# GpSimd waits behind each of the first three choices of a token scatter, not behind the second alone

## The reference

```python
shared = silu_and_mul(x @ shared_gate_up_w.T) @ shared_down_w.T
shared = shared * sigmoid(x @ sgate_w.T)
routing_weights = softmax(x @ gate_w.T)
topk_w, topk_ids = top_k(routing_weights, 4)
for e in range(16):
    coef = sum(where(topk_ids == e, topk_w, 0.0), axis=-1)
    h = silu_and_mul(x @ w13[e].T)
    acc = acc + (h @ w2[e].T) * coef[:, None]
out = shared + acc
```

## Time and profile before

| | us |
|---|---|
| median of 3 runs (lowest and highest) | 1221.72 (1220.41 to 1223.15) |
| the profiled execution: its own time | 1234.23 |
| the profiled execution: span from first to last instruction | 1232.4 |
| TensorE busy in the span | 1166.8 (95%) |
| GpSimd busy in the span | 601.7 (49%) |
| mean granted TensorE clock | 0.984 |

### The profile page before, as it was taken

How to read it: one execution, slowest core, us unless ns; L and a number is a source line. 1 busy time by engine, 2 the same in 40 slices (tenths; PEclk the granted TensorE clock), 3 DMA queues, 4 the chain that set the end, 5 groups by cost and what they waited for, 6 DMA issues and landing times.

```text
span 1232.4 us, 23046 instructions
## 1 busy us (share of the span) xinstructions
PE 1166.8 (95%) x7484; PEld 1003.6 (81%) x7484; DVE 806.7 (65%) x2038; ACT 752.4 (61%) x1734; POOL 601.7 (49%) x497
## 2 busy tenths in 40 slices
PE   6999999999988799988999999999999998989997
PEld 5888888888777577767999999999999996767775
DVE  7867667777784333377777777777777778533335
ACT  5866667666643233336878888888788776323331
POOL 3211222122116356633777766767676752745563
PEclk9999999999999899999999999999999999989999
DMA  3366766663246577651422222212222213666666
GB/s 116 88 175 176 182 156 170 189 172 68 68 147 237 160 132 137 124 122 39 88 76 60 74 62 60 60 62 66 60 66 72 49 47 108 230 210 116 111 112 147
DMA packets 94897, 141.59 MB, mean 115 GB/s; under 512 B 8292, under 2 KB 74084, under 8 KB 94180
## 3 DMA queue, kind: packets, MB, share of 16 engines
q1 hardware_dynamic: 74400, 102.32, 30.6%
q0 software_dynamic: 15744, 20.98, 10.1%
q10 hardware_dynamic: 4676, 17.30, 4.4%
HBM read 99.71 MB, written 40.86 MB: 114 GB/s over the span
## 4 chain that ended last, share of the span: by engine, by line
PE 82%; DVE 7%; DMA 3%; ACT 3%; issue 2%; another core or an unknown queue 1%; POOL 0%; SPq 0%; DVEq 0%; ACTq 0%
PE ps L276 19%; PE ps L278 19%; PE ps L277 19%; PE ps L1123 9%; PE ps L1148 6%; DMA rows_a<-a_rows_d 3%; PE ps L1136 2%; PE ps L551 2%; PE ps L1100 2%; DVE valT L762 1%; PE ps L1697 1%; PE ps L565 1%; DVE ln_st L391 1%; DVE x L1436 1%
## 5 line engine op out<-in xcount | busy, mean ns | idle before, releaser
L1308 POOL DMA_INDIRECT sums_d<-e_y,xg x88 | 137.5, 1563 | 114.2 <-ACT e_y L1233 60.1
L1123 PE MATMUL ps<-w,e_xT 128*128 (+1 forms) x376 | 128.9, 465 | 2.2 <-ACT e_xT L1216 0.9
L1429 DVE COPY e_hT<-ps 88x256 f32<-88x256 f32 x94 | 39.5, 420 | 126.1 <-PE ps L1136 118.5
L427 POOL TENSOR_TENSOR aw_lo<-aw_raw,aw_hi 128x512 fp32r<-128x512 f32 x32 | 42.2, 1320 | 152.3 <-ACT aw_hi L423 152.3
L276 PE MATMUL ps<-xn_hi,aw_hi 128*128 128x512 f32 x256 | 111.2, 435 | 2.4 <-DVE bmat_lo L790 2.4
L857 DVE TENSOR_TENSOR m_a<-ps,e_a 128x384 f32<-128x384 f32 x128 | 71.2, 556 | 58.5 <-PE ps L551 58.0
L278 PE MATMUL ps<-xn_hi,aw_lo 128*128 128x512 f32 x256 | 101.4, 396 | 0.0
L277 PE MATMUL ps<-xn_lo,aw_hi 128*128 128x512 f32 x256 | 100.9, 394 | 0.0
L1148 PE MATMUL ps<-w,e_hT 88*128 (+1 forms) x376 | 96.4, 379 | 0.0
L656 ACT COPY late<-ps 128x256 f32<-128x256 f32 x128 | 47.8, 373 | 69.5 <-PE ps L278 69.4
L1302 POOL DMA_INDIRECT slots_d<-rows,slot_i x64 | 65.4, 1022 | 47.5 <-DVE slot_i L1494 24.0
(11 more groups left out here) (311 smaller groups left out, 4132.7 us busy)
## 6 DMA issues: line engine op xcount, KB each, us to landing
rows_a<-a_rows_d SPq DMA_DIRECT2D x64, 256.0 KB, 5.0
xg<-slots_d SPq DMA_DIRECT2D x94, 144.0 KB
slots_d<-slot_init SPq DMA_DIRECT2D x10, 1152.0 KB, 6.8
wconv_raw<-b_conv SPq DMA_DIRECT2D x16, 513.0 KB
aw_raw<-a_heads SPq DMA_DIRECT2D x32, 256.0 KB, 3.0
wvo_raw<-b_vo SPq DMA_DIRECT2D x16, 512.0 KB
rows_b<-b_rows_d SPq DMA_DIRECT2D x32, 256.0 KB, 4.9
w<-moe_up ACTq DMA_DIRECT2D x4, 1408.0 KB
```

What stands on the lines that cost most here:

```text
L427: return nc.gpsimd.tensor_tensor(dst[1], src, f32(dst[0]), ALU.subtract).then_inc(sem(done_sem), 1)
L1123: ins = nc.tensor.matmul(ps[:, 2 + t % 2, 0:2 * E_HIDDEN], e_xT[:, t % 2, k], weights_of(w13, t, at_w, k * 2 * E_HIDDEN, 2 * E_HIDDEN), st ...
L1308: nc.gpsimd.indirect_dma_start(sums_d[f][t % CHAINS], bass.IndirectOffsetOnAxis(ap=xg[:, t % XG, ROW_ID:ROW_ID + 1].bitcast(U32), axis=0), ...
L1429: nc.vector.tensor_copy(e_hT[0:HALF_E, t % 2], ps[0:HALF_E, 4 + t % 2, 0:2 * P].rearrange("p (j m) -> p j m", j=2)).then_inc(sem("e_hT"), 1)
```

## The change

GpSimd waits for the landing of the eight scatters of choice `i - 1` ahead of each of the choices with `i` = 1, 2 and 3; before, it waited so only ahead of `i` = 2. Nothing else differs. The function runs once in each FFN, so two waits are added in each.

```diff
             for i, k in enumerate(reversed(range(TOP_K))):
-                if i == TOP_K // 2:
+                if i > 0:
                     pool.wait_ge(sem(f"slots_stored{i - 1}"), 16 * BLOCKS * (f + 1))
                 for b in range(BLOCKS):
```

## The result

| | before | after |
|---|---|---|
| median, both run on one chip, 4 runs each (us) | 1221.07 | 1237.89 |
| lowest and highest (us) | 1218.83 to 1223.15 | 1235.58 to 1241.44 |
| ratio, with its 95% interval | | 1.0127 [1.0106, 1.0147] |
| the profiled execution: its own time, span (us) | 1234.23, 1232.4 | 1237.35, 1235.5 |
| mean granted TensorE clock | 0.984 | 0.977 |

The two profiled spans are 3.1 us apart, the medians 16.8. The profile of after is an execution like the timed ones (1237.35 beside 1237.89); the one of before was 13.2 us above the median of this table (12.5 above the first three of its runs). So the two pages can't be subtracted from each other. The rows of after are read against that one.

What follows compares the result with a forecast made beforehand. PE was taken as the bound, with 82% of the chain; tile 3's load delays of 7.9 and 4.6 us hid in slacks of 14.2 and 6.4. So 1234.23 + 0, less 12.5, gave 1221.7, said as 1222.0; range 1218.5 to 1227.0.

Steps and rivals of the forecast that it cites:

- PE is at the shared expert until about 420 and 1097: Scatter stretches of both FFNs: PE works on the shared expert until then, turning tile 3 only at 427.65 and 1105.21.
- Tiles 0 to 2 are loaded long before: SP's tile loads: tiles 0 to 2 arrive before PE finishes the shared expert, so only tile 3 can come late.
- The slack of tile 3, 14.2 and 6.4 us: Between tile 3's load and its turn on PE: slack hiding the forecast delays of 7.9 and 4.6 us.
- The length of a drain: GpSimd's wait from a choice's last issue until its rows land: 1.5 to 4.4 us, from the trace's six landings.
- The fixed cost of about 2.0 us: GpSimd's DMA path: each drain pays about 2.0 us, giving 4.0 us of delay per FFN, hidden too.
- An idle time there that ends with the load of `xg` would be the exposed case, and would have its like in the time: PE ahead of tile 3's turn: none expected; idle time ending with that load would lengthen the run alike.
- GpSimd's idle time ahead of the first sum: GpSimd behind its last scatter: shrinks from 11.16 to about 5 us, so the sums start no later.
- Rival 1: PE reaches tile 3 earlier in timed runs, exposing 4.4 us together: 1226.1; exposed case mean about 1225, chance 0.29.
- Rival 2: Drains calm the shared expert's phase, removing one ACT stall in three, 3.4 us: 1218.3, chance 0.17.

Runs made afterwards that it cites:

- e1: The kernel before, unchanged, run and profiled once more: 1224.01 us, 1.0008 of the kernel before.
- e13: The changed kernel again, on a chip where the stalls are usual: 1236.04 us, 0.9964 of the kernel before.
- e8: The changed kernel with the weights of experts 8 to 11, and 12 and 13 with them, loaded later: 1231.89 us, 1.0082 of the kernel before.
- e6: The kernel before with 120 idle matmuls on PE ahead of tile 0 in each FFN: 1257.19 us, 1.0276 of the kernel before.
- e7: The changed kernel with 120 idle matmuls on PE ahead of tile 0 in each FFN: 1257.52 us, 1.0281 of the kernel before.
- e12: Waits behind all three choices in the first FFN, as before in the second, on a chip with stalls: 1234.13 us, 0.9955 of the kernel before.
- e9: The kernel before with no wait in the scatter loop, on a chip with stalls: 1252.01 us, 1.0118 of the kernel before.
- e2: The kernel before with only the wait behind choice 1 added (waits behind 1 and 2): 1226.75 us, 1.0029 of the kernel before.
- e3: The kernel before with only the wait behind choice 3 added (waits behind 2 and 3): 1229.00 us, 1.0046 of the kernel before.
- e5: The changed kernel run once more, on a chip without stalls: 1236.00 us, 1.0107 of the kernel before.
- e15: The kernel before with only the wait behind choice 3 added, on a chip with stalls: 1234.75 us, 0.9911 of the kernel before.
- e11: Two waits in the loop, each for the choice before the last, on a chip with stalls: 1254.53 us, 1.0130 of the kernel before.
- e18: The changed kernel with weights of experts 8 to 15 loaded later, on a chip with stalls: 1240.23 us, 0.9993 of the kernel before.

## Why the prediction was wrong

1222.0 was forecast, in a range up to 1227.0; it became 1237.89. The steps, in their order:

- **"PE is at the shared expert until about 420 and 1097", "Tiles 0 to 2 are loaded long before".** This is the step that failed. It was true of the one profiled execution, whose stalls (18.8 and 10.9 us of ACT's "remote" waits) had put PE back: it turned tile 0 at 419.25 and 1095.99. In `e1` that is 402.40 and 1080.16, and PE waits 6.16 and 7.36 us for tile 2. Tile 2 was on the path already, behind the drain that exists. In the profile of before, the stall hid it.
- **The slack of tile 3, 14.2 and 6.4 us.** It follows from that step. In `e1` its load is issued at 412.51; with the 2.1 us of the prediction (which hold because the load of a tile waits also for the landing of the tile four before it) it is there at 414.6, and PE turns it at 419.45: 4.8 us in the first FFN. Against the load's delay in after, 421.75 - 412.51 = 9.24 us, that leaves 4.4; measured are 4.88 until the turn.
- **The length of a drain, "1.5 to 4.4 us".** Under-sized: 3.45, 6.71 and 4.94, 3.71, 5.31 and 5.51 in after, up to 7.17 in `e13`. The bound came from three landings in each FFN, read as the time until SP went on. (In the second row the backlog is gone at the 27th digit, not the 25th, which changes little.) The old drain, 3.50 and 1.74 in the profile of before, is 4.92 and 6.77 in `e1`, when PE and ACT keep their pace and the weights meet it. The fixed cost of about 2.0 us in "DMA: Bandwidth & Descriptors" of the Trainium skill (Anatomy of one DMA) agrees with the drain of 1.74 us that `e8` shows with little traffic beside it, and is 0.3 to 0.6 of what the drains of after cost (6.71 to 3.45).
- **"An idle time there that ends with the load of `xg` would be the exposed case, and would have its like in the time".** Right: 24.5 us in six waits beside 13.5 in two. `e6` and `e7` make it a cause: PE late, no price to be seen.
- **The clock** was in no term of the sum. Behind the waits it is 0.55, and the products there take about 2.2 us more in the first FFN alone.
- **GpSimd's idle time ahead of the first sum, "from 11.16 to about 5 us".** It is 0.30. In `e1` it is 6.98, so there was less of it, and the drains took it all.
- **Rival 1, "Tile 3 comes late in runs that aren't profiled".** The right mechanism with the right sign, and with its condition met: "timed runs reach tile 3 several us sooner". Its price, up to 9.5 us, was short, since it gave back only 12.5 us of idle time in proportion, while tile 0 is turned 16.9 us sooner in `e1`; since it left tile 2 out; and since its drains were too short. It took the stalls for the profiler's; `e1` to `e8` were profiled and have none, most of the later profiles have them, so they go with the chip or its state and not with profiling.
- **Rival 2, "The drains calm the shared expert's phase".** False for the result: its runs of before, at 1221 us, are as fast as those of the chips without stalls, which leaves none to calm. True of the stalls where they are usual: `e12` and `e13`, against `e9`. The argument against it, that the stream gets longer and not thinner, doesn't hold.

The two waits together cost more (1.07 and 1.27%) than the two singles add up to (0.75%), by the point values; the intervals of the singles are wide. From the turn of tile 0 to the copy of tile 3, both FFNs together, the singles add 4.2 us (`e2`) and 3.8 (`e3`), and both together 14.4 (after) and 14.7 (`e5`). The account that fits is the 4.8 us of tile 3: one delay is partly absorbed by it, two are not, and the low clock comes on top. That step is argued from the rows, not isolated in a run.

Left open: what holds up PE and ACT on some chips. The runs show when (mostly well into a row of scatters without a drain) and what mostly prevents it (a drain every eight), not which resource it is, nor whether the empty queue or the pause matters; `e15` and the first FFN of `e12` contradict an exact count. Also open: whether the changed kernel is faster or equal on such a chip.

## What to carry to other kernels

Before reading a slack from a profile, compare the time of the profiled execution with the median; where it is 12.5 us longer, the idle time that separates them is just what a slack is made of, and a second profile is worth more than any sum. A wait that empties a DMA queue costs the landing under the traffic of that moment (1.7 us beside little traffic, up to 7.2 beside the weights), so price it by the heaviest traffic that can meet it. And ask of each transfer that waits in a row, not of the last alone, whether the bound engine already waits for it.

## What was not expected of the hardware

- On some chips, PE and ACT are held up while GpSimd issues a long row of scatters by indirect DMA: PE starts one or two instructions in about 1.4 us, ACT waits for up to 20.87 us at a time (`e11`, second FFN), 25 to 30 us per FFN without drains, and 0 to 5 us with a drain every eight scatters (`e12`'s first FFN, `e13`, `e18`). In `e9` from 386 to 408 no weights and no instructions are loaded beside them. The same program took 1223 us where the stalls are absent and 1240 where they aren't.
- With a part of the weights moved away, a drain falls from 6.71 to 1.74 us with the same eight scatters ahead of it (`e8`).
- After a wait of 3.46 us behind one of 8.15, the granted clock is 0.55 from 425 to 431, and four products of 128x352 take 2.55 us, where they take 1.45 at 1.00.
